# Two causal attention stages re-staged: maxima by phases of four heads and 512 queries, rows placed by DMA

## The reference, cut to what matters

```python
scores = jnp.einsum('bhqd,bhkd->bhqk', q, k) * (1.0 / math.sqrt(HD))
causal = jnp.triu(jnp.ones((s, s), dtype=bool), k=1)
scores = jnp.where(causal, -jnp.inf, scores)
attn = jax.nn.softmax(scores, axis=-1)
out = jnp.einsum('bhqk,bhkd->bhqd', attn, v)
```

## Time and profile before

| | us |
|---|---|
| median of three runs | 1035.71 |
| profiled execution | 1038.35 |
| its span on the core | 1036.6 |
| PE busy | 825.3 (80%) |
| DVE busy | 662.0 (64%) |
| ACT busy | 439.3 (42%) |
| first attention stage, maxima and exponentials | 92.1 to 256.9 |

### The profile page before, as it was taken

The page is one execution under the profiler, slowest core; times in us unless marked ns, Lnnn a source line. Parts: engine busy times, 40 slices in busy tenths (PEclk is TensorE's granted clock), DMA queues, the critical chain, the costliest instruction groups (busy, mean ns, idle before and its releaser), DMA issues. The chain is left out here.

```text
span 1036.6 us, 13091 instructions
## 1 busy us (share of the span) xinstructions
PE 825.3 (80%) x4290; PEld 507.2 (49%) x4290; DVE 662.0 (64%) x1738; ACT 439.3 (42%) x868; POOL 197.3 (19%) x356
## 2 busy tenths in 40 slices
PE   1525798999669976798988699666989999938797
PEld 1422223332558853233323579655556666627686
DVE  5687787780765477788862688745227774256575
ACT  4022267778332151377777453244112222224453
POOL 0533013323010022012322000010601222100053
PEclk9757599999979986599999899876999999969899
DMA  7106400000000056300000700089211111040001
GB/s 236 40 4 230 136 1 1 2 1 1 1 1 1 1 172 213 117 1 1 2 1 1 118 1 1 1 292 376 103 45 31 47 47 41 26 128 1 0 1 41
DMA packets 48568, 63.81 MB, mean 62 GB/s; under 512 B 11542, under 2 KB 33814, under 8 KB 48502
## 3 DMA queue, kind: packets, MB, share of 16 engines
q1 hardware_dynamic: 46630, 57.85, 18.1%
q0 software_dynamic: 1872, 5.13, 1.4%
HBM read 50.30 MB, written 15.51 MB: 63 GB/s over the span
## 5 line engine op out<-in xcount | busy, mean ns | idle before, releaser
L669 ACT ACTIVATE at1probs<-at1scores 128x512 f32<-128x512 f32 (+3 forms) x192 | 83.3, 510 | 28.4 <-PE at1scores L604 27.1
L669 ACT ACTIVATE at0probs<-at0scores 128x512 f32<-128x512 f32 (+3 forms) x192 | 83.3, 510 | 28.0 <-PE at0scores L604 26.7
L960 PE MATMUL f2ps<-gu_raw,f2xT_b 128*128 x184 | 82.9, 593 | 1.0 <-ACT f2xT_b L1035 1.0
L1053 ACT ACTIVATE f2sg<-f2ps 128x512 f32<-128x512 f32 x31 | 18.5, 597 | 137.1 <-PE f2ps L960 100.9
L581 PE MATMUL at1scores<-ks,qs 96*128 96x512 bf16 (+1 forms) x192 | 65.4, 382 | 11.3 <-DMA ks<-scratch 4.9
L581 PE MATMUL at0scores<-ks,qs 96*128 96x512 bf16 (+1 forms) x192 | 65.4, 382 | 11.3 <-DVE at0mx L709 4.6
L709 DVE CUSTOM_DVE_ANT_0 at0scores<-at0scores,at0later 128x128 f32<-128x128 f32 (+3 forms) x128 | 61.2, 505 | 11.7 <-PE at0scores L581 11.5
L709 DVE CUSTOM_DVE_ANT_0 at1scores<-at1scores,at1later 128x128 f32<-128x128 f32 (+3 forms) x128 | 61.2, 504 | 11.7 <-PE at1scores L581 11.5
L604 PE MATMUL at1scores<-qs,ks 99*128 99x512 bf16 (+3 forms) x192 | 57.6, 341 | 10.9 <-ACT at1probs L669 7.4
L604 PE MATMUL at0scores<-qs,ks 99*128 99x512 bf16 (+3 forms) x192 | 57.5, 340 | 10.9 <-ACT at0probs L669 7.4
L697 POOL TENSOR_SCALAR_AFFINE_SELECT at1probs<-at1probs 128x128 f32<-128x128 f32 x128 | 36.3, 292 | 126.6 <-ACT at1probs L669 124.5
(11 more groups left out here) (397 smaller groups left out, 1896.6 us busy)
## 6 DMA issues: line engine op xcount, KB each, us to landing
gu_raw<-in_L_ffn_w_gate_up SPq DMA_DIRECT2D x8, 1024.0 KB, 12.7
scratch<-parts SPq DMA_DIRECT2D x8, 768.0 KB, 4.1
qs<-scratch SPq DMA_DIRECT2D x48, 128.0 KB, 2.7
ks<-scratch SPq DMA_DIRECT2D x48, 128.0 KB, 2.7
dn_raw<-in_L_ffn_w_down SPq DMA_DIRECT2D x8, 512.0 KB, 12.2
f2x_in<-slots_in SPq DMA_DIRECT2D x23, 129.0 KB, 2.1
slots_in<-in_c_empty SPq DMA_DIRECT2D x1, 2944.0 KB, 17.3
traw<-in_L_ffn_w_gate_up SPq DMA_DIRECT2D x1, 2048.0 KB, 11.9
```

The costliest lines, as they stand in the source:

```text
L669: act.activation(probs[:, u % NP, 0:n], unit_bank(u, last)[:, 0:n], ACT.Exp, scale=HD ** -0.5)\
L960: ins = pe.matmul(o, xT_b[:, a % 2, k, :], w, start=(k == 0), stop=(k == KD - 1))
L1053: act.activation(sg[:, u % 2, :], ps[:, u % 2, :], ACT.Silu).then_inc(sgs, 1)
```

## The change

Only `attention_stage` and the tables ahead of it change.

- The maxima are taken in 8 phases, (g, qc): four heads and 512 queries. A unit is one head's 128 queries against all their keys, 128 to 512 in a phase of qc = 0 and 640 to 1024 in one of qc = 1; it has one of two buffers of two banks. Units run over the heads within a query tile. VectorE reduces the first 512 keys without mask where there are more, then the rest with the mask.
- A phase's 16 maxima per query are split once, in five operations (qc = 0) or six, and turned by one transpose (48 rows x 128) in one of the two buffers. ScalarE copies that to `rows`, and SyncE places it into the query stack by four DMAs of 12 x 128 bf16, one per head.
- The order is a list of items, units and turns, a turn two units behind its phase's last. 21 units and the first turn come ahead of the first score; then each score is followed by one item as long as the maxima are less than LEAD * GH = 16800 columns ahead of the exponentials, and by five units at u = 15. Counted from the code, the turn of phase 1 follows unit 13 of the exponentials, of phase 2 unit 25, of phase 3 unit 53 and of phase 7 unit 147 of 192.
- The exponentials use two banks in all groups. The first score of a phase waits for that phase's four DMAs.
- SyncE reads group 1's stacks first, then places phase 0, reads group 2, places phase 1, reads group 3, and places the rest.

```diff
...
+PHASES = [(g, qc) for g in range(GROUPS) for qc in range(NC)]
+TILES = CH // P
+PER_PHASE = GH * TILES
+STEPS = [(qc, kt) for qc in range(NC) for kt in range((qc + 1) * TILES)]
+NST = len(STEPS)
+NEXP = GH * NST
+NMAX = NC * PER_PHASE
+ROW_LAG, EARLY, LEAD = 2, 5, 4200
...
+def keys_of(n):
+    p, r = divmod(n, PER_PHASE)
+    qc, t = PHASES[p][1], r // GH
+    return (qc * TILES + t + 1) * P
+def queries_of(u):
+    qc, kt = STEPS[u % NEXP // GH]
+    lo = max(qc * CH, kt * P)
+    return lo, (qc + 1) * CH - lo
...
+def interleave():
...
+    units = PER_PHASE * len(PHASES)
+    items = []
+    for n in range(units):
+        items.append(("unit", n))
+        p = (n - ROW_LAG + 1) // PER_PHASE - 1
+        if (n - ROW_LAG + 1) % PER_PHASE == 0 and p >= 0:
+            items.append(("rows", p))
+    items.append(("rows", len(PHASES) - 1))
+    ahead, i, taken = 0, 0, 0
+    first = []
+    while taken < PER_PHASE + EARLY:
+        first.append(i)
+        taken += items[i][0] == "unit"
+        ahead += keys_of(items[i][1]) if items[i][0] == "unit" else 0
+        i += 1
+    after = []
+    for u in range(GROUPS * NEXP):
+        ahead -= queries_of(u)[1]
+        now = []
+        wanted = EARLY if u == PER_PHASE - 1 else ahead < LEAD * GH
+        while wanted and i < len(items):
+            kind, n = items[i]
+            now.append(i)
+            i += 1
+            if kind == "unit":
+                ahead += keys_of(n)
+                wanted -= 1
+        after.append(now)
+    while i < len(items):
+        after[-1 - 8].append(i)
+        i += 1
+    return items, first, after
+ITEMS, ITEMS_FIRST, ITEMS_AFTER = interleave()
+UNITS_UP_TO = [sum(kind == "unit" for kind, _ in ITEMS[:i + 1]) for i in range(len(ITEMS))]
+ROWS_UP_TO = [i + 1 - n for i, n in enumerate(UNITS_UP_TO)]
+ROWS_AFTER = [[ITEMS[i][1] for i in now if ITEMS[i][0] == "rows"] for now in ITEMS_AFTER]
+ROWS_FIRST = [ITEMS[i][1] for i in ITEMS_FIRST if ITEMS[i][0] == "rows"]
...
+        nm, rest = (sb(n, [P, GH, TILES]) for n in ("nm", "rest"))
+        mst = sb("mst", [P, 2, GH, MP, TILES], BF16)
+        rows = sb("rows", [MP * PER_PHASE, 2, P], BF16)
+        ps_s = pb("ps_s", [P, 2, N])
+        ps_e = pb("ps_e", [P, TB, CH])
+        ps_v = pb("ps_v", [P, NC, CH])
...
-            def max_chunk(g, n, first):
-                j, (qt, c) = n // len(MAX_CHUNKS), MAX_CHUNKS[n % len(MAX_CHUNKS)]
-                if not (first and n < SB):
-                    pe.wait_ge(s_red, g * NMAX + n - SB + 1)
-                n_keys = min(CH, (qt + 1) * P - c * CH)
-                pe.matmul(ps_s[:, n % SB, 0:n_keys], qs[0:STK, g, j, qt * P:qt * P + P],
-                          ks[0:STK, g, j, c * CH:c * CH + n_keys], start=True, stop=True).then_inc(s_full, 1)
...
-            def scores(g, u, first, last):
-                j, (qc, kt) = u % GH, STEPS[u // GH]
-                if u == 0:
-                    pe.wait_ge(m_placed, g * GH + GH)
-                banks = TB + SB if last else TB
-                if last and TB <= u < banks:
-                    pe.wait_ge(s_red, (g + 1) * NMAX)
-                elif not (first and u < TB):
-                    behind = TB if u < TB else banks
-                    pe.wait_ge(exp_done, g * NEXP + u - behind + 1)
...
+            def free(i):
+                if i >= 2:
+                    if ITEMS[i - 2][0] == "unit":
+                        pe.wait_ge(s_red, UNITS_UP_TO[i - 2])
+                    else:
+                        pe.wait_ge(m_out, ROWS_UP_TO[i - 2])
...
+                free(i)
+                keys, qt = keys_of(n), qc * TILES + t
+                q = qs[0:STK, g, j, qt * P:qt * P + P]
+                for lo in range(0, keys, CH):
+                    hi = min(lo + CH, keys)
+                    ins = pe.matmul(ps_s[:, i % 2, lo:hi], q, ks[0:STK, g, j, lo:hi], start=True, stop=True)
+                ins.then_inc(s_full, 1)
+            def max_rows(i, p):
+                pe.wait_ge(m_split, p + 1)
+                free(i)
+                turned = ps_s[0:MP * PER_PHASE, i % 2, :].bitcast(BF16)[:, 0:P]
+                pe.transpose(turned, mst[:, p % 2].rearrange("p j i t -> p (j i t)"), m.identb[:]).then_inc(m_turned, 1)
...
+            def scores(u):
+                g, j = u // NEXP, u % GH
+                qc, kt = STEPS[u % NEXP // GH]
+                if j == 0 and kt == 0:
+                    pe.wait_ge(*rows_place(g * NC + qc))
+                if u >= TB:
+                    pe.wait_ge(exp_done, u - TB + 1)
+                lo, n = queries_of(u)
+                pe.matmul(ps_e[:, u % TB, 0:n], ks[0:ROWS, g, j, kt * P:kt * P + P], qs[0:ROWS, g, j, lo:lo + n],
                           start=True, stop=True).then_inc(st_full, 1)
...
+                if kt == 0 and g > 0:
+                    pe.wait_ge(pv_evac, (g - 1) * NC + qc + 1)
                 for j in range(GH):
...
+            for i in ITEMS_FIRST:
+                item(i)
...
+            for u in range(UNITS):
+                scores(u)
+                for i in ITEMS_AFTER[u]:
+                    item(i)
+                if u % GH == GH - 1 and u >= GH:
+                    values(u // GH - 1)
+            values(GROUPS * NST - 1)
...
-            def place_max(g, j):
-                act.wait_ge(m_trans, g * GH + j + 1)
-                act.activation(qs[STK:STK + MP, g, j, :], ps_m[STK:STK + MP, :], ACT.Copy).then_inc(m_placed, 1)
+            def rows_out(p):
+                act.wait_ge(m_turned, p + 1)
+                if p >= 2:
+                    act.wait_ge(*rows_place(p - 2))
+                i = ITEMS.index(("rows", p))
+                turned = ps_s[0:MP * PER_PHASE, i % 2, :].bitcast(BF16)[:, 0:P]
+                act.activation(rows[:, p % 2, :], turned, ACT.Copy).then_inc(m_out, 1)
...
+            for p in ROWS_FIRST:
+                rows_out(p)
+            for u in range(UNITS):
+                g, n = u // NEXP, queries_of(u)[1]
+                act.wait_ge(st_full, u + 1)
+                if u % GH == 0 and u // GH >= 2:
+                    act.wait_ge(pv_done, u // GH - 1)
+                act.activation(probs[:, u % NP, 0:n], ps_e[:, u % TB, 0:n], ACT.Exp, scale=HD ** -0.5).then_inc(exp_done, 1)
+                for p in ROWS_AFTER[u]:
+                    rows_out(p)
+                if u % NEXP == 2 * GH - 1 and g > 0:
+                    copy_out(g - 1, 1)
+                if u % NEXP == (TILES + 2) * GH - 1:
+                    copy_out(g, 0)
+            copy_out(GROUPS - 1, 1)
...
+            def maximum(i, n):
+                p, r = divmod(n, PER_PHASE)
+                t, j = divmod(r, GH)
+                dve.wait_ge(s_full, n + 1)
+                if keys_of(n) > CH:
+                    dve.tensor_reduce(mx[:, p % 2, 1, j, t:t + 1], ps_s[:, i % 2, 0:CH], AX.X, ALU.max)
+                last = ps_s[:, i % 2, (keys_of(n) - 1) // CH * CH:keys_of(n)]
+                width = (keys_of(n) - 1) % CH + 1
+                dve.tensor_tensor_reduce(last, last, later[:, CH - width:CH], 1.0, -3.0e38, ALU.add, ALU.max,
+                                         mx[:, p % 2, 0, j, t:t + 1]).then_inc(s_red, 1)
+            def split_max(p):
+                dve.wait_ge(s_red, (p + 1) * PER_PHASE)
+                if p >= 2:
+                    dve.wait_ge(m_turned, p - 1)
+                high, middle, low = (mst[:, p % 2, :, k, :] for k in range(MP))
+                if PHASES[p][1] == 0:
...
-            def split_max(g, j):
-                dve.wait_ge(s_red, g * NMAX + 12 * j + 12)
-                c.base, c.n = (g * GH + j) * 4 + 1, 0
-                c.step(dve.tensor_reduce(nm[:], mx[:], AX.X, ALU.max, negate=True))
-                c.step(dve.tensor_copy(mst[:, j, :, 0], nm[:]))
-                c.step(dve.tensor_tensor(rest[:], nm[:], mst[:, j, :, 0], ALU.subtract))
-                c.step(dve.tensor_copy(mst[:, j, :, 1], rest[:]))
-                dve.tensor_tensor(mst[:, j, :, 2], rest[:], mst[:, j, :, 1], ALU.subtract).then_inc(m_split, 1)
...
+                    c.step(dve.tensor_tensor(nm[:], mx[:, p % 2, 0], mx[:, p % 2, 1], ALU.max))
+                    c.step(dve.tensor_scalar(nm[:], nm[:], -1.0, None, ALU.mult))
+                c.step(dve.tensor_copy(high, nm[:]))
+                c.step(dve.tensor_tensor(rest[:], nm[:], high, ALU.subtract))
+                c.step(dve.tensor_copy(middle, rest[:]))
+                dve.tensor_tensor(low, rest[:], middle, ALU.subtract).then_inc(m_split, 1)
...
         def _(sp):
-            for n in range(2, 4):
-                sp.wait_ge(m.written[n], 16)
-            for g in range(1, GROUPS):
+            def read_group(g):
                 sp.wait_ge(m.stacked, g * STACK_SIGNALS)
                 for w in range(2):
                     read_stack(sp, m, g, w)
+            def place(p):
+                g, qc = PHASES[p]
+                sp.wait_ge(m_out, p + 1)
+                for j in range(GH):
```

(51 more changed lines are left out.)

124 lines of the change are left out of this document (37 added, 87 removed).

## The result

The changed kernel takes **1062.38 us** (median of 4 runs, 1056.62 to 1067.11), the one before 1035.15 beside it: ratio 1.026, 95% interval 1.020 to 1.032. It is slower by 27 us, where 1010 and a gain of 26 were forecast. The profiled execution took 1067.11 us with a span of 1065.3, 28.8 more than the profiled one of before. The first stage lost 18.1 us (last copy-out at 275.05 instead of 256.94), the second 13.4 (418.7 to 596.8, 178.1 us, against 398.9 to 563.6, 164.7); the rest of the kernel is some 3 us shorter.

A forecast was written before the change was run, and what follows sets the result against it. Bounds: VectorE in the lead-in, the two-bank loop of TensorE and ScalarE in middle groups. Per stage 18.4 gained, 4.9 lost, 8.6 gained, 7.8 lost, given as 13.0, 26 in all: 1010 us, range 996 to 1026.

The forecast's parts named there:

- First exponential: End of the first stage's lead-in: ScalarE starts at 108.6 instead of 126.97 us, 18.4 us gained.
- The 17th exponential: Start of group 0's second phase, after VectorE's maxima, chain, turn and phase 1's rows: at 127.0 us.
- I put this at under 1 us: Cost of half clock on TensorE beside group 0's first 16 exponentials: under 1 us, inside the range.
- Group 0: First group of a stage, from its first exponential: 41.1 us against 36.2 before, 4.9 us lost.
- Groups 1 and 2: Middle groups of a stage: loop of 30.8 us plus small terms, 31.9 us each, 8.6 us gained.
- Buffers go from three of one bank to two of two banks: Maxima buffers: unit times cover the matmuls except for 128 keys; 0 to 2 us per stage, 1 taken.
- the check of the loop: Middle group before: 30.8 us of two-bank loop plus 2.4 transposes, 1.5 copies and 1.3 group end, 36.0 for measured 36.2.
- Last group: Last group of a stage, on two banks: 30.4 us against 22.7 before, 7.8 us lost.
- Banks of scores: Last group loses five banks and runs the two-bank loop, priced at 2.75 us per full step.
- C: Rival: row DMAs come late in every phase, not two; up to 43 us in all, 1053; chance 0.10, 0.02 at full price.
- A: Rival: the two-bank loop gets no shorter, groups 1 to 3 take 36.2 us each, 1042; chance 0.09.
- B: Rival: VectorE sets the end throughout, the loop hides beside it; 978 at best, half way 996; chance 0.13 for at least half.

The follow-up runs named there:

- the ring: Changed kernel with its four maxima banks as a ring of single banks, signalled and freed bank by bank, instead of two double buffers: 1038.8 us, ratio 1.003.
- ring and six banks: Changed kernel with maxima banks as a ring of single banks and six banks for the exponentials from number 148 on: 1018.8 us, ratio 0.985.
- the unread matmuls on that kernel: Changed kernel with single-bank ring and six late exponential banks, plus 30 matmuls per stage that nothing reads, beside group 0: 1016.3 us, ratio 0.980.
- the same edit: Kernel before with two banks instead of five in its last group, nothing else changed: 1059.0 us, ratio 1.023.
- the run with short transposes: Kernel before with one of a head's eight transposes and a copy of 128 instead of 1024 columns for groups 1 to 3: 1024.1 us, ratio 0.989.
- six banks: Changed kernel, double buffers kept, with six banks for the exponentials from number 148 on: 1041.0 us, ratio 1.006.

## Why the prediction was wrong

The sign was wrong and the measured time lies 36 us above the upper end of the range. Point by point, first stage:

- **First exponential**: 109.1 against 108.6. Right, with the chain 0.25 us below and the transfers 0.5 us above their prices.
- **The 17th exponential**: 131.2 against 127.0. The step let VectorE run freely up to the turn of phase 1; from 109 to 127 us it is busy 14.9 of 18 us, and the granted clock is 0.69. "I put this at under 1 us" was too little, though no run separates this part from the buffers: the ring took 19.6 us for these sixteen, not 22.1.
- **Group 0**: 50.7 against 41.1, of which the ring alone removes 4.4. It stays at 46 with the ring. What holds these last 5 us is not settled. VectorE is busy 33.1 of the 38 us from 107 on with ring and six banks. The clock may have a part too: the unread matmuls on that kernel raised group 0's granted clock from 0.83 to 0.96 in the second stage, and the group took 43.4 instead of 45.5 us; in the first stage the clock rose only from 0.82 to 0.86, and the group stayed at 45.8.
- **Groups 1 and 2**: 38.5 and 39.5 against 31.9. The step that failed is "Buffers go from three of one bank to two of two banks ... nothing to 2 us per stage, I take 1, at the start". It compared a matmul with a unit's time, engine by engine. For VectorE's chains the forecast had TensorE's own wait at the turn (1.0 us in a group), and not what follows from it: two buffers hold two items of any size, also where an item is 128 keys or a turn, so that with VectorE away for a chain nothing more can be laid ready for it. The ring measured this term at 23.6 us in all, 11.8 per stage, against 1 (group 0's part of it, of a cause not settled, is in this figure). A second part is the check of the loop: its other terms gave 36.0 for 36.2 and so looked proven, but the run without them gave back half. The 36.2 was too high besides: from first exponential to first exponential, groups 1 and 2 took 35.4 in the kernel before. A sum that closes doesn't show that its terms would all go.
- **Last group**: 37.3 against 30.4. "Banks of scores. The last group loses its five banks and runs the two-bank loop" was priced at the full clock, 2.75 us a step. At the full clock it measured 2.88; at the lower level, which held for two of these steps and the narrower ones ahead of them, 4.2. On the kernel before the same edit took 36.9 us for the group where 22.2 stood, 14.7 us (13.4 in the second stage), where the forecast's own steps (30.4, without 1.7 for the last turn) made it 6.5. The earlier trace rows had the warning: the lead-in, thin work with waits, was granted 0.50.
- Where the sum went: 0.5 + 9.6 + 6.6 + 7.6 + 6.9 is the 31.2 us between 243.9 and 275.1.
- The forecast's own balance had a slip that did not touch its time: 18.4 - 4.9 + 8.6 - 7.8 is 14.3 and not 13.0 per stage. It set groups cut at the first exponential against groups of before cut at the first score and evenly (36.2, 22.7). Cut alike, by the table above, it is 18.4 - 4.2 + 7.0 - 8.2 = 13.0.

**Of the rivals**, C at its full price (1053) was nearest in number and wrong in cause: rows were late in two phases, as forecast. A (the pace of the groups doesn't fall, 1042) came nearest in kind: it named the sign and the point of about 35.5 us, and the run with short transposes bears out its ground by half; but it did not see the groups get slower than before, and had no term for the clock. B did not happen. The mark given in the text worked: groups 1 and 2 over 35 us was stated as the sign of a wrong forecast.

The plan of the change was sound. With a ring instead of double buffers, six banks at the end and a larger lead, its first stage ends at 245.4 and the kernel takes 1009.0 us, about the forecast's 243.9 and 1010: partly by chance, since group 0 is 9 us longer and the last group 8 shorter than in the forecast.

## What to carry to other kernels

Count buffers in time, not in bytes: for each, ask how long its consumer may be away (a chain, a copy, a long item) and whether what is in flight covers that; signalling and freeing by the smallest piece was worth 23.6 us here. When a change takes buffers from a stretch that ran without a gap, price the loop at both levels of the clock, since the loop on two banks ran partly at the lower one here, and on five banks not at all. And test a model of a loop by taking one of its terms away before trusting all of them.

## What the runs showed that was not expected

- TensorE stayed at the lower level of its clock through a loop in which it is counted busy nearly all the time. Kernel after, two 512 steps, then the next two:

```profile
253.80:262.20 8.40, 7.88 (x26) 1.09 (x24) 0.00 (x0) 4.83 (x9) 0.00 (x0) 0.50 0.01 2
262.20:268.00 5.80, 4.96 (x26) 0.93 (x24) 0.00 (x0) 4.35 (x9) 1.17 (x4) 0.90 0.00 0
```

  Busy 7.88 of 8.40 us at 1.2 GHz, with an idle piece of 0.26 us in each step; then the same loop mostly at 2.4. So it runs at either level for steps on end, and which one it is in makes 4.2 or 2.88 us. The Trainium skill's page TensorE: Matmul & The Clock Gate (A second HAM failure mode: psum-queue depth-cycling) describes short idle pieces between groups of matmuls, from cycling through PSUM banks, that send the clock back and forth. The trace agrees on the cause, as far as six banks bring the granted clock of the last group from 0.73 (237.8 to 275.05 us) to 0.93 (232.76 to 258.76 us in that run); but in this stretch it didn't swing, it stayed down for several steps and then up.
- Matmuls that nobody reads, 22 per stage, made the last group shorter (33.0 instead of 37.3 us, and 34.1 instead of 36.5), though the 4.5 us by which the median fell are not clear of the spread.
- Four transfers of 3 KB within the chip occupy SyncE's queue for 3.04 us, and the first score that needs them starts 4.24 us after the first issue; the earlier trace rows had suggested 3.6 to landing.
